# Attention probabilities turned by DMA crossbar instead of by TensorE, with exponentials kept in PSUM and three score banks

## What is computed

```python
# x, ctx_1024: (16, 256, 512)
x = x + tanh(g_xattn) * attn(layernorm(x), ctx, Wq, Wk, Wv, Wo, bo)
x = x + tanh(g_ffn) * moe(layernorm(x), router, w_gate, w_up, w_down, shared)
# attn: q = x @ Wq.T; k, v = ctx @ Wk.T, ctx @ Wv.T
scores = einsum("bhqd,bhkd->bhqk", q, k) * SCALE     # causal mask
probs = softmax(scores, axis=-1)
y = einsum("bhqk,bhkd->bhqd", probs, v) @ Wo.T + bo
```

## Time and profile before

| | before |
|---|---|
| median of 3 runs | 1934.5 us (1931.85 to 1935.63) |
| the profiled execution | 1933.8 us, its span 1932.0 us |
| TensorE matmul / weight load busy | 1877.0 us (97%) / 1593.2 us (82%) |
| VectorE busy | 1517.6 us (79%) |
| ScalarE busy | 970.2 us (50%) |
| GpSimd busy | 716.4 us (37%) |
| DMA queue of SyncE | 180.68 MB, 33.2% of 16 engines |

### The profile page before, as it was taken

One profiled execution on the slowest core, in us unless ns is written; L12 is line 12 of the kernel. 1 busy time (PEld: TensorE's weight loads), 2 busy tenths in 40 slices (PEclk: granted clock), 3 DMA queues, 4 the chain that ended last, 5 costly groups with the idle time before them and its releaser, 6 DMA issues.

```text
span 1932.0 us, 33464 instructions
## 1 busy us (share of the span) xinstructions
PE 1877.0 (97%) x11664; PEld 1593.2 (82%) x11664; DVE 1517.6 (79%) x3339; ACT 970.2 (50%) x2284; POOL 716.4 (37%) x945
## 2 busy tenths in 40 slices
PE   6999999999999899999999999999999999999999
PEld 6899998899998778888878888877888886888887
DVE  5888888888888777777778777787777778877776
ACT  4777777777777733334334333343334333423332
POOL 3122233332323443434543344363334454333330
PEclk9999999999999899999999999999999999999999
DMA  7565566555666131121123212114122111312111
GB/s 213 128 149 130 145 154 144 146 144 148 153 144 164 56 120 62 59 88 44 55 73 107 72 55 66 55 33 150 47 77 72 49 55 65 110 55 63 48 44 44
DMA packets 151494, 182.81 MB, mean 95 GB/s; under 512 B 11424, under 2 KB 115872, under 8 KB 151328
## 3 DMA queue, kind: packets, MB, share of 16 engines
q1 hardware_dynamic: 151328, 180.68, 33.2%
HBM read 111.43 MB, written 18.87 MB: 67 GB/s over the span
## 4 chain that ended last, share of the span: by engine, by line
PE 74%; DVE 13%; issue 6%; ACT 3%; POOL 3%; DMA 1%; SPq 1%; DVEq 0%; POOLq 0%
PE gate_up L1234 30%; PE down L1746 18%; PE bank L741 14%; PE probs_t L872 4%; PE scores L842 3%; DVE ops_lo L1091 2%; DVE acc L1599 2%; PE bank L731 1%; POOL hidden L1447 1%; PE y L861 1%; PE y L859 1%; DVE probs L673 1%; PE down L1725 1%; DVE pt_lo L705 1%; ACT probs L556 1%
## 5 line engine op out<-in xcount | busy, mean ns | idle before, releaser
L1234 PE MATMUL gate_up<-xo_hi,ops_hi 128*128 128x512 f32 x1120 | 442.2, 395 | 17.0 <-DVE gated L1210 8.7
L1234 PE MATMUL gate_up<-xo_hi,ops_lo 128*128 128x512 f32 x1120 | 438.5, 392 | 0.0
L1234 PE MATMUL gate_up<-xo_lo,ops_hi 128*128 128x512 f32 x1120 | 438.4, 391 | 0.0
L1234 PEld LDWEIGHTS gate_up<-xo_hi,ops_hi 128*128 128x128 f32 x1120 | 211.8, 189 | 70.0 <-DVE gated L1210 14.1
L1599 DVE SCALAR_TENSOR_TENSOR acc<-down,scale,acc 128x512 f32<-128x512 f32 x320 | 239.1, 748 | 34.7 <-PE down L1746 34.3
L1746 PE MATMUL down<-d_lo,h_hi 128*128 128x512 f32 x640 | 249.0, 389 | 0.0
L1746 PE MATMUL down<-d_hi,h_hi 128*128 128x512 f32 x640 | 249.0, 389 | 0.0
L1746 PE MATMUL down<-d_hi,h_lo 128*128 128x512 f32 x640 | 249.0, 389 | 0.0
L1234 PEld LDWEIGHTS gate_up<-xo_lo,ops_hi 128*128 128x128 f32 x1120 | 211.6, 189 | 44.9
L1234 PEld LDWEIGHTS gate_up<-xo_hi,ops_lo 128*128 128x128 f32 x1120 | 211.9, 189 | 43.0
L1447 POOL TENSOR_TENSOR hidden<-hidden,gated 128x512 f32<-128x512 f32 x120 | 157.2, 1317 | 190.2 <-DVE hidden L1215 170.7
(11 more groups left out here) (179 smaller groups left out, 4605.3 us busy)
## 6 DMA issues: line engine op xcount, KB each, us to landing
g_raw<-in_w_gate SPq DMA_DIRECT2D x40, 512.0 KB, 3.9
u_raw<-in_w_up SPq DMA_DIRECT2D x40, 512.0 KB, 3.9
d_raw<-in_w_down SPq DMA_DIRECT2D x40, 512.0 KB, 3.7
k_stack<-k_hi SPq DMA_DIRECT2D x128, 128.0 KB, 2.6
q_stack<-q_hi SPq DMA_DIRECT2D x128, 128.0 KB, 2.6
c_in<-in_ctx_t SPq DMA_DIRECT2D x16, 512.0 KB, 3.8
x_in<-in_x SPq DMA_DIRECT2D x16, 512.0 KB, 3.7
k_stack<-k_lo SPq DMA_DIRECT2D x64, 128.0 KB, 2.6
```

The source lines that it names most:

```text
L1234: ins = pe.matmul(gu_ps[bank][:], ops[x][:, which, a, c, :], xo[y][:, b, c, :], start=(begins and c == 0 and i == 0), stop=(c == CH - 1 an ...
```

## The change

- The probabilities stay in PSUM. There are three banks `sc_ps` of 512 columns each: 128 for the first 128 queries (128 keys; the masked half of that block isn't computed any more) and 256 for the others. Mask and exponentials work in place there.
- One slot after the scores (`SPLIT_LAG`) ScalarE copies them as float16 into `halves[.., 0, :]`, and VectorE writes the rest into `halves[.., 1, :]`: the split comes before the turn. There are three such buffers.
- SyncE issues one DMA with `transpose=True` per head, 128x768 of float16, from `halves` into one of four buffers `turned`. The values matmuls read `turned`; their lag goes from 4 to 5 slots.
- The two banks `pt_ps` are gone. One bank `rows_ps` serves all turns of rows: `x_in`, `y` and, four blocks in one go at slot 13, `x_hat`; ScalarE copies those with one instruction at slot 14.
- TensorE waits for the low part of three heads back before it writes a score bank.
- SyncE's queue is ordered by slot: a turn in each, the stacks three to a slot in slots 5 to 8 and 9 to 12, and the loads at slots 2, 3 and 14; the store of `x1` moves to slot 0 of the iteration after.
- Layernorm work moves: statistics of `x_in` from slot 5 to 7, normalising from 13 to 10, moments of `x_hat` from 3 to 0, their inverse root from 4 to 2.

```diff
-    RING = 4
-    probs = [sb(f"probs{i}", [P, 3 * P]) for i in range(RING)]
-    pt_hi = [sb(f"pt_hi{i}", [P, 3 * P], F16) for i in range(2)]
-    pt_lo = [sb(f"pt_lo{i}", [P, 3 * P], F16) for i in range(2)]
+    RING, TURNED = 3, 4
+    halves = [sb(f"halves{i}", [P, 2, 3 * P], F16) for i in range(RING)]
+    turned = [sb(f"turned{i}", [P, 2, 3, P], F16) for i in range(TURNED)]
...
-    sc_ps = [psum(f"scores{i}", [P, T, S]) for i in range(2)]
-    pt_ps = [psum(f"probs_t{i}", [P, D]) for i in range(2)]
+    sc_ps = [psum(f"scores{i}", [P, P + 3 * P]) for i in range(RING)]
+    rows_ps = psum("rows_t", [P, D])
...
-    TR_LAG, PV_LAG = 2, 4
+    SPLIT_LAG, PV_LAG = 1, 5
+    RES_LOAD, X_LOAD, C_LOAD, ROWS_LOAD = 2, 3, 14, 14
+    K_STACK, Q_STACK = (5, 6, 7, 8), (9, 10, 11, 12)
-    LN_SLOT, C_SLOT, XN_SLOT = 5, 12, 13
-    RES_SLOT, MOMENTS_SLOT, STD_SLOT, HAT_SLOT = 6, 3, 4, 6
-    HAT_FIRST, HAT_T_SLOT = 4, H - C
+    LN_SLOT, C_SLOT, XN_SLOT = 7, 12, 10
+    RES_SLOT, MOMENTS_SLOT, STD_SLOT, HAT_SLOT = 6, 0, 2, 6
+    HAT_FIRST, HAT_T_SLOT, HAT_T_EVAC = 4, 13, 14
...
+            def turn(k):
+                wait(sp, pv_done, k - TURNED + 1)
+                sp.sem_inc(sp_passed, 1)
+                sp.wait_ge(p_lo_made, k + 1)
+                sp.dma_start(turned[k % TURNED][:].rearrange("p x t q -> p (x t) q"), halves[k % RING][:].rearrange("p x k -> p (x k)"),
+                             transpose=True).then_inc(p_turned[k % TURNED], DMA)
...
+                for s in range(H):
+                    if (bh := lagging(i, s, SPLIT_LAG)):
+                        turn(head(*bh))
...
+                    if s in K_STACK and has(i, 1):
+                        j = K_STACK.index(s)
...
                         stack(k_stack[par], j, 0, k_hi).then_inc(stacked[par][j], DMA)
                         stack(k_stack[par], j, 1, k_hi).then_inc(stacked[par][j], DMA)
                         stack(k_stack[par], j, 2, k_lo).then_inc(stacked[par][j], DMA)
...
+                    if (bh := lagging(i, s, SPLIT_LAG)):
+                        k = head(*bh)
+                        if k >= RING:
+                            act.wait_ge(p_turned[(k - RING) % TURNED], DMA * ((k - RING) // TURNED + 1))
+                        act.wait_ge(probs_made, k + 1)
+                        act.copy(halves[k % RING][:, 0, :], probs_of(k)).then_inc(p_hi_made, 1)
...
+                    if (bh := lagging(i, s, SPLIT_LAG)):
+                        k = head(*bh)
+                        dve.wait_ge(p_hi_made, k + 1)
+                        dve.tensor_tensor(halves[k % RING][:, 1, :], probs_of(k), halves[k % RING][:, 0, :],
+                                          ALU.subtract).then_inc(p_lo_made, 1)
...
-                        wait(pe, max_made, i.times(H, s - 1))
+                        wait(pe, p_lo_made, head(i, s) - RING + 1)
                         pairs = slice(0, 3 * DH)
                         for t in range(T):
-                            ins = pe.matmul(sc_ps[s % 2][:, t, :], q_stack[par][pairs, s, tile(t)],
-                                            k_stack[par][pairs, s, :], start=True, stop=True)
+                            keys = slice(0, P * (t + 1))
+                            ins = pe.matmul(scores_of(head(i, s), t), q_stack[par][pairs, s, tile(t)],
+                                            k_stack[par][pairs, s, keys], start=True, stop=True)
...
-                        pe.wait_ge(pt_lo_made, b.times(H, h + 1))
+                        n_head = head(b, h)
+                        pe.wait_ge(p_turned[n_head % TURNED], DMA * (n_head // TURNED + 1))
+                        p_hi, p_lo = turned[n_head % TURNED][:, 0], turned[n_head % TURNED][:, 1]
...
-                        for k in range(3):
-                            ins = pe.transpose(pt_ps[h % 2][:, tile(k)], probs[h % RING][:, tile(k)], ident[:])
-                        ins.then_inc(pt_done, 1)
                     units(i, s)
+                    if s == HAT_T_SLOT and hat_tile(i) is not None:
+                        k = hat_tile(i)
+                        pe.wait_ge(x_hat_made, k + 1)
+                        transpose_rows(lambda c: x_hat[:, k % T, c * P:(c + 1) * P], rows_ps).then_inc(hat_t_done, 1)
```

More of the change, by code:

```diff
@@ L319, in hat_tile, with scores_of, probs_of @@
         return k if 0 <= k < HATS * T else None
+    def scores_of(k, t):
+        return sc_ps[k % RING][:, P:2 * P] if t == 0 else sc_ps[k % RING][:, 2 * P:]
+    def probs_of(k):
+        return sc_ps[k % RING][:, P:]
     def is_last(i):
@@ L327, in is_end, with y_bank, head @@
         return isinstance(i.r, int) and i.k == B
+    def y_bank(i, t):
+        return bank[1 - t] if is_end(i) else rows_ps
+    def head(b, h):
+        return b.k * H + h
     def phase(i):
@@ L368, in run @@
                 k = hat_tile(i + -1)
[L369 to L381, removed]
@@ L396, in run @@
                         stack(k_stack[par], j, 2, k_lo).then_inc(stacked[par][j], DMA)
-                if phase(i) == 0:
-                    start.sync(sp, phase(i), 1)
-                if has(i, 1):
-                    sp.wait_ge(q_lo_made, n.times(2, 2))
-                    for j in range(JH):
+                    if s == K_STACK[-1] and phase(i) == 0:
+                        start.sync(sp, phase(i), 1)
+                    if s in Q_STACK and has(i, 1):
+                        j = Q_STACK.index(s)
+                        if j == 0:
+                            sp.wait_ge(q_lo_made, n.times(2, 2))
                         stack(q_stack[par], j, 0, q_hi).then_inc(stacked[par][j], DMA)
@@ L563, in run @@
                         normalise_rows(hat_tile(i))
+                    if s == HAT_T_EVAC and hat_tile(i) is not None:
+                        keep_hat(hat_tile(i))
                     if phase(i) >= 0:
@@ L781, in units @@
                         pe.wait_ge(xn_made, n.times(T, t + 1))
-                        if t == 0:
-                            wait(pe, x1_made, n.times(T, 2 - 3 * T))
-                        else:
-                            pe.wait_ge(k_lo_made, n.times(2, 1))
-                        transpose_rows(lambda c: x_in[:, t, c * P:(c + 1) * P], bank[X_BANKS[t]]).then_inc(xt_done, 1)
+                        if t == 0 and hat_tile(i + -1) is not None:
+                            pe.wait_ge(hat_t_made, hat_tile(i + -1) + 1)
+                        if t == 1:
+                            pe.wait_ge(xt_lo_made, n.times(T, 1))
+                        transpose_rows(lambda c: x_in[:, t, c * P:(c + 1) * P], rows_ps).then_inc(xt_done, 1)
                     if s in Q_SLOTS:
@@ L801, in units @@
                                 pe.wait_ge(q_lo_made, n.times(2, 1))
-                            elif half == 0 and has(i, -1):
-                                pe.wait_ge(yt_lo_made, o.times(T, 1))
                             elif half == 0:
@@ L826, in units @@
                                 pe.wait_ge(yt_lo_made, o.times(T, T))
-                            elif half == 0 and has(i, 1):
-                                pe.wait_ge(v_rest_made, n.times(T, T))
+                            if half == 0 and has(i, 1):
+                                pe.wait_ge(v_rest_made, n.times(T, t + 1))
+                            elif half == 0:
+                                wait(pe, x1_made, o.times(T, t + 1 - T))
                             ins = three_pass(bank[t][:], rows(t_hi, t_lo, tile(t)), weight(WO), HALF_CHUNKS[half])
```

169 lines of the change are left out of this document (82 added, 87 removed).

## The result

| | before | after |
|---|---|---|
| median of 4 runs each | 1933.33 us | 2030.19 us (2027.91 to 2030.93) |
| ratio | | 1.0495, 95% interval 1.0482 to 1.0508 |
| span of the profiled execution | 1932.0 us | 2029.2 us |
| TensorE busy | 1877.0 us, 97% | 1841.9 us, 91% |
| VectorE busy | 1517.6 us | 1512.1 us |

The direction is that of the forecast, the size is not: +97 us where +38 was given.

The account below looks back on a forecast made before the run. TensorE bound the kernel, VectorE close behind; after the change SyncE's queue would. Span 1932.0 + 34 (15.5 batches x 2.2) + 3 (end) = 1969; with +1.8 for the profiled execution and 0.7 for the median, 1972 us; range 1872 to 2160.

Parts of the forecast that it names:

- (A): The forecast case: SyncE's queue binds in slots with stacks, T 0.9 to 1.7 us, 1940 to 2050 us; chance 0.40.
- One of its signs: Spacing of heads expected under (A): 3.1 us apart in slots with stacks and 2.25 elsewhere.
- T: Issue cost of one turn on SyncE's queue, taken as 1.1 us by pieces, bounds 0.37 and 3.6 us.
- The rule of the Trainium skill: Rule against crossbar turns: 1309 ns per 128x128 block, six in a row for a head 7.9 us.
- 8 x 3.1 - 1.3 + 8 x 2.25: Batch period: eight stack slots at SyncE's 3.1 us, 1.3 slack once, eight at 2.25: 41.5 us, 2.2 more than now.
- The pace where nothing else binds: TensorE and VectorE together, nearly equally loaded: 36.0 us per batch, 2.25 per head, 35.2 at best.
- The wait for stored rows: Moved layernorm work, moments of stored rows from slot 3 to 0: covered by other work while VectorE has idle time.
- (B): Rival of cheap turn issues, T 0.37 to 0.7 us: 1886 us at 0.37, 1910 at 0.6; chance 0.37.
- TensorE's removed turns: Turns of probabilities deleted from TensorE's queue: 16 heads x 0.28 = 4.5 us per batch saved.
- Scores of 128 columns: First scores matmul of a head on TensorE: taken as 0, range -1.0 to +1.9 us per batch.
- Masks and exponentials in PSUM: In-place writes by VectorE and ScalarE: taken as 0, a tenth either way, up to 1.1 us per batch on VectorE.
- DMA engines: Turns add 15.7 us to 22.7, 38.4 us of engine work per batch; in stack slots 2.5 us, below 3.1.

Follow-up runs that it names:

- e12: Changed kernel with one stack DMA of three issued from the third batch on, 8 per batch instead of 24: 1944.49 us.
- e4: Changed kernel with each stack DMA moving an eighth of its columns from the third batch on, as many issues: 2024.97 us.
- e11: Changed kernel with five buffers of halves, six of turned, values lag six, and moments of stored rows back at slot 3: 2010.25 us.
- e8: Changed kernel with only the high half of the probabilities turned, half the bytes and pieces per turn: 2013.74 us.
- e13: Changed kernel with two heads per turn, three pair buffers of halves, two of turned, moments of stored rows at slot 3: 1978.64 us.
- e10: Changed kernel with plain copies for turns, five buffers of halves, six of turned, values lag six, moments at slot 3: 1925.09 us.
- e9: Changed kernel with moments of stored rows back from slot 0 to 3 and their inverse root from 2 to 4: 2022.77 us.
- e7: Kernel before with one edit, the first scores matmul of a head reading 128 keys instead of 256: 1932.51 us.
- e14: As e13 but two pair buffers of halves, three of turned, and values six slots behind: 1971.52 us.
- e15: As e14 with the stack DMAs' bytes cut to an eighth from the third batch on, as many issues: 1955.15 us.

## Why the prediction was right in its cause and wrong in its size

**The cause.** (A) named SyncE's queue as the new bound, and the turn's wait on ScalarE as the place where it shows. Both are in the trace, and e12 against e4 and the full queue of e11 show the first. The crossbar DMA takes 1.256 us of issue, where 0.9 to 1.7 was given for this case. One of its signs did not come: heads were to be 3.1 us apart in slots with stacks and 2.25 elsewhere, and are 2.6 and 3.0.

**How T was reached** was wrong all the same. The forecast scaled it by pieces, 768 x 1.45 ns. e8, after, and e13 have 384, 768 and 1536 pieces at minima of 1.18, 1.21 and 1.27 us: 0.06 us for 768 more. The cost is nearly fixed per DMA. The trace of the kernel before could have told so much: its 0.37 us is that of the context load (line 409), which has 512 pieces of 1 KB, while the loads of `x_in` with their 256 pieces of 2 KB take the same 0.37. That the number fell near is luck, and the error mattered: a cost by pieces would have made two heads per turn useless, while it recovers about half of the loss.

**The rule of the Trainium skill** (VectorE: DVE Perf Modes, "The three transpose paths", 1309 ns for one block of 128x128) doesn't add up by blocks here: six blocks are issued in 1.256 us and land 2.7 us after the issue at the least (3.6 in the middle), far below 7.9. What the Trainium skill says elsewhere, that such DMAs are as fast as plain ones (Advanced Engine Details and Errata, "X-Bar Transpose (TRN2)"), doesn't hold for the issue: 1.26 us against 0.52 for a plain copy of the same bytes. For the way from issue to landing the traces are near it: 3.8 us in e11 against 3.3 for the plain copy in e10.

**The step that failed: 8 x 3.1 - 1.3 + 8 x 2.25, the period, 41.5 us forecast, 45.25 measured.** It charged SyncE's queue only in the eight slots with stacks, let it fall behind by 1.3 us once, and gave the other eight slots the pace of the engines, 18.0 us. Measured, those eight take 24.0 us and the eight with stacks 21.1 instead of 23.5. The queue falls behind by up to 6.2 us while the stacks go out, and the slots behind them pay. What holds is the queue's sum over the whole batch, 42.9 us of 45.25. The forecast's own entries for that sum are 17.5 + 16 x 1.15 = 35.9 us. The 7.0 us between are the turns (21.2 instead of 17.6), the other issues (3.1 instead of 1.9; the loads of x rows went from 0.37 to 0.57 us each) and the short gaps (3.1, of which it had only 0.8).

The difference of 3.75 us times 15 batches is 56 of the 60 us between the spans of forecast (1969) and trace (2029.2); the last batch is the other 4 (3 forecast, 6.8 measured). In the forecast's own formula it can be booked like this. With the mean T of 1.32 it gives 8 x (1.95 + 1.32 + 0.05) - 1.3 + 18.0 = 43.3. The pace where nothing else binds was put at 2.25 us a head, 36.0 a batch. e10 shows 38.2, 2.39 a head: +1.1 in the formula, 44.4. The wait for stored rows, which I had counted among moves that other work covers, is 45.25 - 44.4 = 0.8 us (e9, period (614.7 - 126.1)/11): 45.2. That the sum closes proves little, since the slots don't divide as the formula has it.

**The pace was wrong as well,** and it carried (B). I took two equal loads, 34.8 us for TensorE and 34.5 for VectorE, and added 1.2 us for their not meeting. The plain copy with deep buffers has both about 90% busy and adds 3.4 us to the higher load; what those are was not shown. Had it been right, the case of cheap turns would have gained 2.5%; measured, its best is 0.45%.

**Smaller steps.** TensorE's removed turns: they are gone, but TensorE no longer binds, so nothing was gained. Scores of 128 columns, taken at 0 with bounds on both sides: 0 (e7). Masks and exponentials in PSUM, taken at 0: 5 and 44 ns dearer on VectorE, up to 50 ns cheaper on ScalarE. DMA engines: I forecast 38.4 us of work per batch and called it no bound; their share is 0.98 at 45.25, 44 us, and yet e4 shows no bound. My reading is that the share counts also time in which packets wait for one another, for it comes to 1.04 in e14, and a busy share can't pass 1; no run separates that. Their work becomes part of the bound once the issues are fewer (e15). The clock: in the stretch from 700 to 751 us, which holds the last batch, the granted clock was 0.60, so for most of it TensorE ran at the lower of its two levels, 1.2 GHz, and it was busy for 33.0 us of 51. The last batch of the kernel before had 0.77 and 25.3 us of 30. How much of the 6.8 us the clock has was not separated. In the ten steady batches it was 0.98, so it isn't what cost the 90 us.

```profile
700.00:751.00 51.00, 33.04 (x240) 26.36 (x241) 33.20 (x112) 31.01 (x102) 26.90 (x18) 0.60 0.79 162
```

```profile
625.00:655.00 30.00, 25.30 (x229) 20.98 (x228) 23.30 (x91) 26.06 (x84) 17.44 (x13) 0.77 0.11 36
```

## What to carry to other kernels

Before work is moved to DMAs, add up the issues of the queue that gets them over a whole period, gaps included, at the mean duration of that very form of DMA; a queue can be full of issues while its DMA engines are not (a share of 0.70 in e4). A crossbar turn cost about 1.2 us of its queue here whether it had 96 or 192 KB, and 1.5 with 384, so turn as much as fits at once. And where a second engine stands at the same load as the bound, as here, run the cheap stand-in (the plain copy) first, for it gives the ceiling of the gain.

## What the runs showed of the hardware that I had not expected

- The issue of a DMA transpose on SyncE takes 1.18, 1.21 and 1.27 us at the least for 96, 192 and 384 KB (1.21, 1.26 and 1.48 in the middle); a plain DMA of 192 KB takes 0.46 at the least, and 0.59 when cut into 768 pieces.
- A stack issue takes 0.60 us with pieces of 1 KB and of 128 bytes alike (e4), though the context load with more pieces (512 of 1 KB) takes 0.42.
- The same load need not cost the same issue: the 512 KB loads of x rows take 0.37 us in the kernel before and 0.57 after.
- Scores matmuls with 128 columns instead of 256 take no less of TensorE's queue: 0.24 us for the pair both ways.
- A DMA share of 0.98 isn't a bound by itself: with seven eighths of the stacks' bytes left out it was 0.70, and the time within 5 us of the same (e4).
